# The first layer's bias as a two-row matmul, and silu and its slope formed from z in PSUM, in the gradient stage

## What is computed

```python
def _mlp(w1, b1, w2, b2, x):
    return jax.nn.silu(x @ w1.T + b1) @ w2.T + b2
def loss_fn(params):
    pred = _mlp(*params, k_flat)
    return 0.5 * jnp.sum((pred - v_flat) ** 2)
grads = jax.grad(loss_fn)((w1, b1, w2, b2))
upd = jax.tree_util.tree_map(lambda p, g: (1.0 - alpha) * p - theta * g, (w1, b1, w2, b2), grads)
```

## Time and profile before

| | |
|---|---|
| median of three runs | 2858.36 us |
| the profiled execution, whole | 2876.44 us |
| its span, first to last instruction | 2874.5 us |
| mean granted clock of TensorE | 0.958 |
| busy share of the span | PE 88%, DVE 70%, POOL 53%, ACT 43% |
| gradient stage | 504 to 1728 us |
| its steady iterations, p = 1 to 31 | 541.17 to 1676.93 us |

### The profile page before, as it was taken

How to read it: one execution, slowest core, us unless ns; L and a number is a source line. 1 busy time by engine, 2 the same in 40 slices (tenths; PEclk the granted TensorE clock), 3 DMA queues, 4 the chain that set the end, 5 groups by cost and what they waited for, 6 DMA issues and landing times. The chain is left out here.

```text
span 2874.5 us, 40441 instructions
## 1 busy us (share of the span) xinstructions
PE 2527.2 (88%) x15410; PEld 2230.8 (78%) x15410; DVE 2017.6 (70%) x3738; ACT 1240.4 (43%) x2159; POOL 1517.8 (53%) x901
## 2 busy tenths in 40 slices
PE   7899997688888888888888889999999679989997
PEld 6787786577777777777777777777777578888897
DVE  6888885677777777777777775767666545555554
ACT  4777776323333332223233325555555333333342
POOL 2434432455555555555555543666666446566666
PEclk9999999799999999999999999999999789999999
DMA  3222211500000000000000013223222033433331
GB/s 122 67 82 67 89 45 57 217 23 23 23 23 23 23 23 23 23 23 23 23 23 23 10 45 106 89 96 96 96 78 62 18 104 119 137 117 109 117 118 57
DMA packets 135360, 189.31 MB, mean 66 GB/s; under 512 B 13506, under 2 KB 104167, under 8 KB 135168
## 3 DMA queue, kind: packets, MB, share of 16 engines
q1 hardware_dynamic: 121344, 156.29, 16.9%
q0 software_dynamic: 13824, 30.44, 3.2%
HBM read 122.16 MB, written 72.12 MB: 68 GB/s over the span
## 5 line engine op out<-in xcount | busy, mean ns | idle before, releaser
L651 POOL TENSOR_TENSOR prob<-prob,softmax_small 128x1024 f32<-128x1024 f32 x65 | 124.1, 1909 | 237.0 <-DVE softmax_small L574 237.0
L1905 POOL TENSOR_TENSOR m_hl<-m_hf,m_hh 128x512 fp32r<-128x512 f32 x112 | 168.6, 1516 | 146.4 <-ACT m_hh L1613 146.3
L102 PE MATMUL g_bank<-dpred_h,h_l 128*128 128x256 f32 x520 | 158.9, 306 | 81.8 <-DVE shared_x L1179 42.5
L1277 POOL TENSOR_TENSOR shared_x<-shared_x,silu_q 128x1024 f32<-128x1024 f32 x33 | 79.7, 2415 | 275.6 <-DVE silu_q L1132 275.6
L102 PE MATMUL g_bank<-halves_h,w2T_l 128*128 128x256 f32 (+1 forms) x528 | 169.2, 320 | 62.9 <-DVE halves_l L1140 62.9
L1277 POOL TENSOR_TENSOR silu_slope<-silu_slope,silu_q 128x1024 f32<-128x1024 f32 x32 | 77.0, 2407 | 261.2 <-DVE silu_q L1132 261.2
L2273 POOL TENSOR_TENSOR e_hl<-e_hf,e_hh 128x640 fp32r<-128x640 f32 x96 | 153.4, 1598 | 89.9 <-DVE e_hh L2231 89.5
L2231 DVE CAST e_hh<-e_hf 128x640 fp32r<-128x640 f32 x128 | 108.4, 856 | 118.8 <-ACT e_hf L2169 118.8
L102 PEld LDWEIGHTS g_bank<-dpred_h,h_l 128*128 128x128 f32 x520 | 104.5, 201 | 90.6 <-DVE shared_x L1179 46.3
L1917 POOL DMA_INDIRECT xbuf_d<-xn,scatter_rows x128 | 150.2, 1173 | 45.3 <-issue 38.9
L102 PEld LDWEIGHTS g_bank<-halves_h,w2T_l 128*128 128x128 f32 x528 | 118.2, 224 | 69.7 <-DVE halves_l L1140 69.7
(11 more groups left out here) (285 smaller groups left out, 9388.5 us busy)
## 6 DMA issues: line engine op xcount, KB each, us to landing
shared_x<-in_x SPq DMA_DIRECT2D x32, 512.0 KB, 4.8
shared_xT<-xT_d SPq DMA_DIRECT2D x64, 256.0 KB, 4.5
new_w1T<-in_W SPq DMA_DIRECT2D x16, 1024.0 KB, 5.3
new_w2T<-in_W SPq DMA_DIRECT2D x16, 1024.0 KB, 5.8
xbuf_d<-new_w1T SPq DMA_DIRECT2D x16, 650.0 KB, 8.4
slots<-xbuf_d SPq DMA_DIRECT2D x16, 650.0 KB, 6.9
xn_d<-xn SPq DMA_DIRECT2D x32, 256.0 KB, 2.5
xT_d<-shared_xT SPq DMA_DIRECT2D x32, 256.0 KB, 2.4
```

The costliest lines, as they stand in the source:

```text
L102: i = e.matmul(out, a, b, start=first and n == 0, stop=last and n == len(terms) - 1)
L651: e.tensor_tensor(p[:], p[:], sm[:, 3].unsqueeze(2).broadcast_to([P, HEADS, 2 * P]), ALU.mult).then_inc(*prob_made(g))
L1277: e.tensor_tensor(t[:], t[:], qf[:], ALU.subtract).then_inc(*slope_made(g))
L1905: e.tensor_tensor(hl[:, t], hf[(HC * C + t) % NZ][:], hh[:, t], ALU.subtract).then_inc(*h_low(C, t))
```

## The change

The bias no longer is added by DVE. At the start of the stage six small DVE instructions turn the bias (the first two of its 128 equal rows) into `b1_rows`, two rows of 1024 in fp32r of which one is the high half and the other the low half, and fill `ones`, two rows of 128 ones. For each bank of z, PE first runs one matmul with two rows of contraction, ones by b1_rows, 512 columns, and then the six matmuls of before on top of it. So there are two more matmuls a tile, four a pair, 130 in all.

ACT takes the sigmoid from z in PSUM. DVE forms h = z s from PSUM (two halves), and then `rest` = (z + 1) - h from PSUM (two halves), where silu_q was. POOL multiplies the slope buffer by rest. z's bank is free only when rest is made. There are two rest buffers, the second in the shared_xT buffer that held the bias, so DVE waits for the slope of two tiles back and not of the last tile. The low half of the residual (`rest_dT`) moves on DVE from the end of `residual` to behind add_w1 0. At the end of the stage SP loads an old weight into rest in place of silu_q, and the second chunk waits for the last slope.

```diff
@@ tensor: forward
                 for i, hc in enumerate(cols):
+                    pe.wait_ge(*bias_made.at(5))
+                    pe.wait_ge(*freed("z", g, i))
+                    e.matmul(bank("z", g, i)[:], ones[:], b1_rows[:, hc], start=True, stop=False)
                     pe.wait_ge(*xT_low.at(p))
-                    pe.wait_ge(*freed("z", g, i))
                     matmul_split(e, bank("z", g, i)[:], [(xTh[:, k, block[b]], xTl[:, k, block[b]]) for k in range(KC)],
-                                 [(w1h[:, k, hc], w1l[:, k, hc]) for k in range(KC)]).then_inc(*z_done(g, i))
+                                 [(w1h[:, k, hc], w1l[:, k, hc]) for k in range(KC)], first=False).then_inc(*z_done(g, i))
@@ scalar: forward
-                    act.wait_ge(*z_biased.at(g, i))
+                    act.wait_ge(*z_done.at(g, i))
...
-                    e.activation(sp[g % 4][:, hc], hf[g % 2][:, hc], ACTF.Sigmoid).then_inc(*sig_half(g, i))
+                    e.activation(sp[g % 4][:, hc], bank("z", g, i)[:], ACTF.Sigmoid).then_inc(*sig_half(g, i))
@@ vector: forward
                 for i, hc in enumerate(cols):
-                    dve.wait_ge(*z_done.at(g, i))
-                    dve.wait_ge(*b1_in.at(0))
+                    dve.wait_ge(*sig_half.at(g, i))
                     dve.wait_ge(*hT_done.at(g - 2, 1))
                     dve.wait_ge(*h_low.at(g - 2))
-                    dve.wait_ge(*q_made.at(g - 2))
-                    e.tensor_tensor(hfull[:, hc], bank("z", g, i)[:], b1[:, hc], ALU.add).then_inc(*z_biased(g, i))
+                    dve.wait_ge(*rest_made.at(g - 2, 1))
+                    e.tensor_tensor(hfull[:, hc], bank("z", g, i)[:], t[:, hc], ALU.mult).then_inc(*h_half(g, i))
                 for i, hc in enumerate(cols):
-                    dve.wait_ge(*sig_half.at(g, i))
-                    e.tensor_tensor(hfull[:, hc], hfull[:, hc], t[:, hc], ALU.mult).then_inc(*h_half(g, i))
-                dve.wait_ge(*h_half.at(g, 1))
-                dve.wait_ge(*slope_made.at(g - 1))
-                e.scalar_tensor_tensor(qf[:], t[:], 1.0, hfull[:], ALU.subtract, ALU.mult).then_inc(*q_made(g))
+                    dve.wait_ge(*h_half.at(g, i))
+                    dve.wait_ge(*slope_made.at(g - 2))
+                    e.scalar_tensor_tensor(rest[g % 2][:, hc], bank("z", g, i)[:], 1.0, hfull[:, hc],
+                                           ALU.add, ALU.subtract).then_inc(*rest_made(g, i))
@@ vector: before the loop
+            dve.wait_ge(*b1_in.at(0))
+            e.memset(rest[0][0:2, 0:P], 1.0).then_inc(*bias_made(0))
+            e.tensor_copy(b1_rows[:], b1).then_inc(*bias_made(1))
+            dve.wait_ge(*bias_made.at(0))
+            e.tensor_copy(ones[:], rest[0][0:2, 0:P]).then_inc(*bias_made(2))
+            dve.wait_ge(*bias_made.at(2))
+            e.tensor_tensor(rest[0][0:2], b1, b1_rows[:], ALU.subtract).then_inc(*bias_made(3))
+            dve.wait_ge(*bias_made.at(3))
+            dve.wait_ge(*ident_in.at(0))
+            e.tensor_scalar(rest[0][0:2], rest[0][0:2], ident[0:2, 1:2], None, ALU.mult).then_inc(*bias_made(4))
+            dve.wait_ge(*bias_made.at(4))
+            e.scalar_tensor_tensor(b1_rows[:], b1_rows[:], ident[0:2, 0:1], rest[0][0:2], ALU.mult, ALU.add).then_inc(*bias_made(5))
             rest_xT(0)
@@ vector: in the loop
                 if back:
                     add_w1(p - 1, 0)
+                if now:
+                    rest_dT(p)
+                if back:
                     add_w1(p - 1, 1)
@@ gpsimd: forward
-                pool.wait_ge(*q_made.at(g))
-                e.tensor_tensor(t[:], t[:], qf[:], ALU.subtract).then_inc(*slope_made(g))
+                pool.wait_ge(*rest_made.at(g, 1))
+                e.tensor_tensor(t[:], t[:], rest[g % 2][:], ALU.mult).then_inc(*slope_made(g))
@@ sync: at the end
-                    sp_.wait_ge(*h_half.at(TILES - 1, 1))
+                    sp_.wait_ge(*slope_made.at(TILES - 1))
```

More of the change, by code:

```diff
@@ L806, in gradient_phase @@
         hf = [sb(f"h_full{i}", [P, HID]) for i in range(2)]
-        qf = sb("silu_q", [P, HID])
+        rest = [sb("silu_rest", [P, HID]), shared.xT[1]]
         sp = shared.x + [sb(f"silu_slope{i}", [P, HID]) for i in (2, 3)]
@@ L816, in gradient_phase @@
         ident, row_scale, b2c = sb("g_ident", [P, P]), sb("mem_row_scale", [P, P]), sb("b2_col", [P, KC])
-        b1 = shared.xT[1]
+        b1 = shared.xT[1][0:2]
+        b1_rows, ones = sb("b1_rows", [2, HID], F32R), sb("ones_rows", [2, P], F32R)
         dz_sum = sb("dz_sum", [P, HID])
@@ L857, in gradient_phase @@
         sums_done = signal("sums_done", [0])
-        z_biased, h_half, q_made = signal("z_biased", kinds["z"]), signal("h_half", kinds["z"]), signal("q_made", tiles)
+        h_half, rest_made = signal("h_half", kinds["z"]), signal("rest_made", kinds["z"])
+        bias_made = signal("g_bias_made", range(6))
         hT_low, dz_half = signal("hT_low", kinds["hT"]), signal("dz_half", kinds["dh"])
@@ L888, in freed @@
             kind, *key = use[n]
-            return {"z": z_biased, "hT": hT_low, "pred": dp_made, "dT": dp_low, "dh": dz_half,
+            return {"z": rest_made, "hT": hT_low, "pred": dp_made, "dT": dp_low, "dh": dz_half,
                     "g2": g2_added, "g1": g1_added}[kind].at(*key)
@@ L896, in gradient_phase @@
         old += [(g2[:, 4 * k:4 * k + 4], w2T_v[:, 4 * k:4 * k + 4]) for k in range(2)]
-        old_sb = [t[:] if n < 2 else t[:].rearrange("p (a b) -> p a b", b=D) for n, t in enumerate([qf, *sp[1:]])]
+        old_sb = [t[:] if n < 2 else t[:].rearrange("p (a b) -> p a b", b=D) for n, t in enumerate([rest[0], *sp[1:]])]
         def tensor(e):
@@ L1163, in residual, with rest_dT @@
                     i.then_inc(*mem_scaled(1))
+            def rest_dT(p):
+                N = blocks_of(p) * P
                 dve.wait_ge(*dT_high.at(p))
```

## The result

The changed kernel takes 2757.95 us (median of 4 runs, 2755.19 to 2759.68); the kernel before takes 2858.61 us. The ratio of the mean times is 0.9643, 95% interval 0.9626 to 0.966. The profiled execution took 2757.26 us, with a span of 2755.5 us.

What follows compares the result with a forecast made beforehand. PE was taken as the bound: 36.64 us an iteration less stalls and low clock gives 30.75, plus 2.44 makes 33.19. Over 31 iterations 107 us gained, less 3.5 at the ends: 2755 us, range 2700 to 2802.

Steps and rivals of the forecast that it cites:

- two stalls: PE's waits per iteration before predict (1.75 us) and before accumulate_w2 number 2 (2.64 us), both forecast to go.
- The two-row matmul: Cost on PE of each added bias matmul, including entering and leaving: 0.61 us, four making 2.44 us an iteration.
- stream-only rival: On PE, a two-row matmul costs only its 512-column stream, 0.23 us: 2708 us, chance 0.20.
- PE's own work: PE's steady iteration at full clock without stalls, before adding the two-row matmuls: 30.75 us.
- The term of the low clock: A stretch of PE steps at 1.2 GHz soon after a stall, 1.5 us lost an iteration, forecast to go.
- DVE's passes: DVE's forward step reading PSUM: product 0.68 us and rest 0.74 us each, 2.84 us a tile instead of 6.87.
- The spare time at predict: Margin by which the last rest_hT is done before PE comes to predict: some 0.8 us.
- the rival in which predict still waits: DVE's chain stays late, so PE's stall before predict and the low clock stay: 2856 us, chance 0.08.
- The clock still falls: Rival: PE's stalls go but a 1.2 GHz stretch stays in every iteration: 2801 us, chance 0.15.
- slower by the clock: Rival: two-row matmuls bring PE's clock down for z's six matmuls behind each: 2896 us, chance 0.03.
- The ends: Cost outside the steady iterations, from DVE's setup instructions and first and last iterations: 3.5 us, between 0 and 7.
- From the profile to the median: Profiled execution's 18 us above the median taken as outside this stage, so the median goes from 2858.4 to 2755 us.

Runs made afterwards that it cites:

- e5_before_pool_cut: The kernel before with three of POOL's four steps for a tile cut to 8 of 1024 columns from the fifth tile on: 2683.9 us.
- e1_no_bias: The changed kernel without its 130 two-row matmuls, so the gradient's forward pass leaves the bias out: 2682.5 us.
- e8_late_w2: The changed kernel with one more wait on PE, in accumulate_w2 number 2, for POOL's low half of h: 2886.6 us.
- e9_q_kept: The changed kernel with rest formed the old way, (s - 1) h from SBUF in two halves, and subtracted on POOL: 2849.2 us.
- e11_before_a: The kernel before, unchanged, run again for a second profile: 2859.0 us.

## Why the prediction was right, and where it was off

*What bounds, and the mechanism.* Right: PE with two stalls and a low clock in each iteration, and DVE held by POOL behind the stalls. e5_before_pool_cut shows the cause without the change, e1_no_bias that PE alone is left.

*The two-row matmul.* Forecast 0.61 us from attention's 64-row group, measured 0.63 us. The stream-only rival (0.23 us) is what 128 rows cost.

*PE's own work.* Forecast 30.75 us, measured 30.29 us, so the stalls and the clock cost 0.46 us more an iteration than the sum had. The term of the low clock was right: 1.5 us were put for it, and the two kinds of iteration differ by 1.5 us in e8_late_w2 (35.7 and 37.2), e9_q_kept (35.05 and 36.55) and the kernel before (35.6 and 37.1). What the sum left out is the 0.25 us that each stall costs beyond its idle time (e8_late_w2), and there are two an iteration: 1.75 + 2.64 + 1.5 + 0.5 = 6.4 us, and 36.64 - 30.29 = 6.35 us were there to win. The new iteration was thus put at 33.19 us and is 32.82.

*DVE's passes.* The product takes 0.69 us (forecast 0.68), and rest 0.68 us where line 1713 gave 0.74.

*Stalls.* Both gone. The spare time at predict, put at 0.8 us, is 1.2 us; POOL's, put at 2.1 us, is 3.0 us. So the rival in which predict still waits was not near for the change as it is, but e9_q_kept shows it: one step left in SBUF, 2849 us, where that rival stood at 2856. "The clock still falls" and "slower by the clock" fell with a granted clock of 1.00 in the window.

*The ends.* Put at 3.5 us. The six small instructions cost more than the 4 us that they were put at: they run from 503.94 to 510.48 us (the first cast, of 2 x 1024, takes 2.06 us and that of 2 x 128 takes 1.04 us), and PE's first matmul starts at 510.55 in place of 505.53 us. Iteration 0 gave 1.6 of these 5.0 us back where 0.5 was put, so the first mark is 3.45 us later (541.17 to 544.62). That this meets 3.5 is luck: e8_late_w2 has the same iteration 0, and there the mark is at 545.99 us. Behind the steady part it is 1197.6 us before and 1195.9 us after, but the two other profiles of the kernel before have 1191.8 and 1193.8 us, so that is no gain that the runs show.

*From the profile to the median.* This step failed. Against its own profile the forecast was a gain of 103.5 us and the measured one is 119.2 us (2876.44 to 2757.26), 15.7 us more: 13.8 us in the steady iterations (120.8 in place of 107) and 1.8 us at the ends. Of the 13.8 us, 11.4 are the 0.37 us by which the new iteration is shorter than forecast, and 2.4 the short first one. I then took the 18 us by which that profile lies above the median as lying outside the stage. But e11_before_a, at the median's time, has 9.2 us of them in the very iterations that the change shortens. The gain between medians is 100.7 us. So it was luck that the forecast of 2755 us came within 3 us: a gain put 16 us too small met a profile that stood 18 us too high. The mechanism was right, and the size of the gain was right to some 15%.

## What to carry to other kernels

Where VectorE shares time with GpSimd, count its instructions with two operands in SBUF: each can wait for a whole GpSimd instruction, so move one operand to PSUM, or make one long instruction of several short ones. A matmul of few rows between full ones pays for the change of the row count twice; pad it with zero rows to 128. A short stall of TensorE costs more than its length: one of 2.6 us cost 2.9 us, and 4.4 us where the low clock followed. A profile of a kernel that stalls is one draw from a spread, so set it beside other runs before taking differences.

## What was not expected

A bias matmul of 2 rows costs 0.63 us and one of 128 rows 0.225 us. Two halves of one VectorE step cost 5.00 us beside GpSimd, the whole in one instruction 2.69. After stalls of 2.6 us of the same length the clock fell in some iterations (0.21 us steps for 3.4 us) and in others not at all. The kernels without stalls vary by 3 to 8 us between runs, those with stalls by 6 to 22 us (2852.6 to 2874.8 for the kernel before).
